# Two message-passing layers on a graph: edge maxima made in 13 pieces from flags computed early, and the last gathers' index tables copied by SP

## The reference

```python
h = jnp.maximum(_layernorm(x, axis=-1), 0.0)
# layer 0, with self loops appended to src, dst and ea
m = jax.nn.leaky_relu(x_l[src] + x_r[dst] + e_emb, NEG_SLOPE)
alpha = jnp.einsum('ehf,hf->eh', m, att)
amax = jax.ops.segment_max(alpha, dst, num_segments=n)
ex = jnp.exp(alpha - amax[dst])
denom = jax.ops.segment_sum(ex, dst, num_segments=n)
alpha = ex / (denom[dst] + SM_EPS)
out = jax.ops.segment_sum(x_l[src] * alpha[..., None], dst, num_segments=n)
...
# layer 1
msgs = x[src]
summed = jax.ops.segment_sum(msgs, dst, num_segments=n)
out = summed / jnp.maximum(deg, 1.0)[:, None] @ w_l.T + x @ w_r.T + b
```

## Time and profile before

| | us |
|---|---|
| median of 3 runs | 5774.85 |
| lowest and highest of the 3 | 5769.9, 5776.28 |
| the profiled execution: its time | 5776.47 |
| the profiled execution: its span | 5775.2 |

### The profile page before, as it was taken

One profiled execution on the slowest core, in us unless ns is written; L12 is line 12 of the kernel. 1 busy time (PEld: TensorE's weight loads), 2 busy tenths in 40 slices (PEclk: granted clock), 3 DMA queues, 4 the chain that ended last, 5 costly groups with the idle time before them and its releaser, 6 DMA issues. The chain is left out here.

```text
span 5775.2 us, 78491 instructions
## 1 busy us (share of the span) xinstructions
PE 4011.0 (69%) x16994; PEld 2971.1 (51%) x16995; DVE 3433.7 (59%) x8703; ACT 1190.3 (21%) x4516; POOL 3747.3 (65%) x3701
## 2 busy tenths in 40 slices
PE   5888888888888884699999998444444444334336
PEld 4766666666666663344444456343333333333336
DVE  7666666666666667899999999732222232222224
ACT  2111111111111110466666645200000000000001
POOL 4777777777777772465556540167777777777772
PEclk9999999999999997799999998555555555555555
DMA  8444444444444441243344431211111111111111
GB/s 129 131 133 131 128 131 130 130 130 132 129 130 131 128 130 52 90 112 112 110 111 111 112 83 30 58 24 26 26 26 26 26 26 26 26 26 26 26 26 33
DMA packets 620266, 477.65 MB, mean 83 GB/s; under 512 B 439032, under 2 KB 447352, under 8 KB 619820
## 3 DMA queue, kind: packets, MB, share of 16 engines
q1 hardware_dynamic: 452074, 254.69, 17.3%
q0 software_dynamic: 104800, 108.55, 10.7%
q10 hardware_dynamic: 63202, 112.44, 5.3%
HBM read 350.08 MB, written 125.20 MB: 82 GB/s over the span
## 5 line engine op out<-in xcount | busy, mean ns | idle before, releaser
L509 POOL DMA_INDIRECT ZR<-hD,mS x1664 | 1590.7, 956 | 563.9 <-issue 488.9
L1268 POOL DMA_INDIRECT BIG<-h2D,mS x1564 | 1475.9, 944 | 706.1 <-issue 468.3
L1292 PE MATMUL PS<-BIG,ZR 128*128 x3328 | 809.5, 427 | 1150.4 <-SPq L1245 524.8
L1292 PEld LDWEIGHTS PS<-BIG,ZR 128*128 128x128 f32 x3328 | 738.9, 328 | 1221.1 <-issue 656.1
L539 PE MATMUL PS<-Wz,R 128*128 128x264 f32 x3328 | 1057.2, 400 | 80.1 <-issue 79.5
L567 DVE SCALAR_TENSOR_TENSOR PS<-PS,a 128x528 f32<-128x528 f32 x832 | 596.3, 717 | 798.8 <-PE PS L540 795.0
L804 PE MATMUL PS<-R,ZR 128*128 128x329 f32 x3328 | 1024.8, 469 | 24.0 <-DVE ZR L739 18.4
L540 PE MATMUL PS<-BIG,R 128*128 x3328 | 1028.8, 391 | 0.0
L1311 DVE TENSOR_TENSOR BIG<-BIG,PS 128x64 f32 x1664 | 363.4, 218 | 916.8 <-PE PS L1292 747.1
L790 POOL TENSOR_TENSOR R<-ZR,R 128x768 f32<-128x768 f32 x416 | 615.9, 1480 | 418.7 <-ACT R L776 416.8
L818 DVE TENSOR_TENSOR BIG<-BIG,PS 128x329 f32 x1664 | 814.0, 489 | 11.3 <-PE PS L804 7.2
(11 more groups left out here) (252 smaller groups left out, 2355.1 us busy)
## 6 DMA issues: line engine op xcount, KB each, us to landing
zD<-ZR ACTq DMA_DIRECT2D x416, 256.0 KB, 2.2
ZR<-zD SPq DMA_DIRECT2D x416, 256.0 KB, 2.6
R<-relD SPq DMA_DIRECT2D x105, 512.0 KB
ZR<-ea SPq DMA_DIRECT2D x1664, 32.0 KB
ZR<-hD,mS POOLq DMA_INDIRECT x1664, 2.5
BIG<-h2D,mS POOLq DMA_INDIRECT x1564, 2.4
AL<-hD SPq DMA_DIRECT2D x28, 224.0 KB, 2.8
lmS<-lmD SPq DMA_DIRECT2D x106, 32.0 KB, 1.8
```

What stands on the lines that cost most here:

```text
L509: Q.indirect_dma_start(zring[:, j % 32, 0, :], None, hD, bass.IndirectOffsetOnAxis(mS[:, j // 16, j % 16:j % 16 + 1], 0)).then_inc(hs[q], 16)
L1268: Q.indirect_dma_start(BIG[:, j * F:j * F + F], None, h2D, bass.IndirectOffsetOnAxis(mS[:, (j // 16) % 4, j % 16:j % 16 + 1], 0)).then_inc ...
L1292: ins = P.matmul(bank3(j // 4)[:, j % 4, :], oh[:, (j // 4) % 4, j % 4, :], rows, start=True, stop=True)
```

## The change

**Preparation.** SP stores metaS behind relD and keyD instead of ahead of them, and no longer loads D. The flags (key differs from the last edge's) are computed inside the table product: ACT loads the keys again in tiles of 130 at pair KEYS = 14 (`keys_again`, which waits for the stores of keys and tables), DVE compares, scales and reduces them at pairs 18 to 20 (`flags`), PE and ACT turn and keep them at pairs 21 to 25, ACT's queue stores them at pair 27 and loads at pair 36 the flags of chunks (FLG, 6657 columns, the size of D) and their minima (cmin), which DVE reduces once ahead of sweep 1.

**Edge maxima.** ACT copies by column in 13 pieces and moves the turned pieces; DVE scans each piece as it comes, starting from the last column of the one before. The exchange between chunks is shorter: the flags' minima are there already, and DVE reads PE's result where it is. The second forward scan and the first backward scan are over the whole row. The second backward scan is in 13 pieces (`maxima`), each followed, one piece later, by PE's turn back and by `exponents`: DVE subtracts and masks straight from PSUM, ACT takes the exponential and writes zeros over what is no longer needed. The store of the maxima to lmD follows all pieces. The first loads of sweep 2's destinations stand ahead of the barrier, and behind the store only 3328 columns each are left to zero on DVE and POOL.

**Sweep 3.** SP, in `landings3`, issues a DMA of 16 columns of the index table into mS when it has seen a piece land (flows i3). ACT only copies mR. The wait of PE by register (1291) is as before.

```diff
-    dma(S, metaS.rearrange("a p c -> p a c"), MS.rearrange("p (a c) -> p a c", c=16), dM)
+    sources_turned = sa.n
...
+    S.wait_ge(sa.s, sources_turned)
+    dma(S, metaS.rearrange("a p c -> p a c"), MS.rearrange("p (a c) -> p a c", c=16), dM)
...
+    def keys_again():
+
+        dK.wait(A)
+        dM.wait(A)
+        dma(A, K3, bass.AP(kf.tensor, 0, [[128, 128], [128 * 128, 13], [1, 130]]), dKL)
+
+    def flags(step):
+
+        if step == 0:
+            dKL.wait(V)
+            v(V.tensor_tensor(F3, K3[:, :, 1:130], K3[:, :, 0:129], ALU.not_equal))
+        if step == 1:
+            v(V.tensor_scalar(G2, F2, BIGNEG, None, ALU.mult))
+        if step == 2:
+            v(V.tensor_reduce(tmid, G3[:, :, 1:128], AX.X, ALU.min))
+            for t in range(2):
+                sv.on(V.tensor_tensor(tmin[:, t, :], tmid, G3[:, :, 128 * t], ALU.min))
+            sv.wait(P, A)
...
+        dma(A, flagD[:, 0:NS * 128].rearrange("o (k p e) -> (o p) k e", p=128, e=128), G3[:, :, 0:128], dFl)
+        sa.wait(A)
+        dma(A, fminD.rearrange("t (k p) -> (t k) p", p=128), tmin_t, dFl)
+        dma(A, flagT, FT, dFl)
+
...
+        dFl.wait(A)
+        for t in range(2):
+            dma(A, cmin[:, t, :], bass.AP(fminD[t, :].tensor, NS * t, [[52, 32], [0, 4], [1, 52]]), dFm)
+        dma(A, FLG, bass.AP(ff.tensor, 0, [[CH, 32], [0, 4], [1, CH + 1]]), dD)
...
-    dK.wait(S)
-    dB.wait(S)
-    D, dD = BIG[:, 25998:25998 + CH + 2], dsem()
-    kf = keyD[0, :]
-    for h in range(4):
-        dma(S, D[h:128:4, :], bass.AP(kf.tensor, 0, [[CH, 32], [1, CH + 2]]), dD)
+    dFm.wait(V)
+    v(V.tensor_reduce(fmin, cmin, AX.X, ALU.min))
...
+    def by_column(q):
+        sa.on(A.copy(by_slot(CP[:, cols(q)]), AL4[:, 4 * q:4 * q + 4]))
+        at["cp", q] = sa.n
...
-    v(V.tensor_tensor(Fl, D[:, 1:CH + 2], D[:, 0:CH + 1], ALU.not_equal))
-    v(V.tensor_scalar(Fl, Fl, BIGNEG, None, ALU.mult))
...
-        v(V.tensor_copy(keep[:, 1:2], flags[:, 0:1]))
-        v(V.tensor_reduce(keep[:, 1:2], flags, AX.X, ALU.min))
-        v(V.tensor_tensor_scan(d(out), d(flags), d(data), BIGNEG, ALU.add, ALU.max))
...
+        sa.on(A.copy(AT[:, cols(q)], PS[:, q % 4, :]))
+        at["turned", q] = sa.n
+        if q + 2 < 13:
+            by_column(q + 2)
+        V.wait_ge(sa.s, at["turned", q])
+        before = FWD[:, 512 * q - 1:512 * q] if q else BIGNEG
+        v(V.tensor_tensor_scan(FWD[:, cols(q)], FLG[:, cols(q)], AT[:, cols(q)], before, ALU.add, ALU.max))
+
+    def from_other_chunks(col, t):
...
-    segmented_max(FWD, AT, Fl[:, 0:CH], False)
-    segmented_max(B, FWD, Fl[:, 1:CH + 1], True)
-    v(V.tensor_tensor(AT, AT, B, ALU.subtract))
+        v(V.tensor_copy(ini, PS[:, 6, 0:1]))
+
+    from_other_chunks(FWD[:, CH - 1:CH], 0)
+    v(V.tensor_tensor_scan(FWD, FLG[:, 0:CH], AT, ini, ALU.add, ALU.max))
+    nothing = bc(allone[:, 0:1], [128, 512])
     sv.wait(A)
-    sa.on(A.activation(AT, AT, ACT.Exp))
-    ex_rdy = sa.n
-    v(V.scalar_tensor_tensor(FWD, Fl[:, 1:CH + 1], 0.0, B, ALU.is_lt, ALU.mult))
...
+    for q in range(13):
+        sa.on(A.activation(AT[:, cols(q)], nothing, ACT.Copy, scale=0.0))
+    v(V.tensor_tensor_scan(LM[:, ::-1], FLG[:, 1:CH + 1][:, ::-1], FWD[:, ::-1], BIGNEG, ALU.add, ALU.max))
+    from_other_chunks(LM[:, 0:1], 1)
+    dFS.wait(V)
...
+    def maxima(q):
+
+        after = FWD[:, 512 * q + 512:512 * q + 513] if q < 12 else ini
+        if q < 12:
+            V.wait_ge(sv.s, at["max", q + 1])
+        b = FWD[:, cols(q)][:, ::-1]
+        sv.on(V.tensor_tensor_scan(b, FLG[:, 512 * q + 1:512 * q + 513][:, ::-1], b, after, ALU.add, ALU.max))
+        at["max", q] = sv.n
+        P.wait_ge(sv.s, sv.n)
+        if q + 4 < 13:
+            P.wait_ge(sv.s, at["lm", q + 4])
...
+        at["back", q] = sp.n
+
+    def exponents(q):
+
+        V.wait_ge(sp.s, at["back", q])
+        c, m = slice(4 * q, 4 * q + 4), by_slot(PS[:, q % 4, :])
+        sv.on(V.tensor_tensor(AL4[:, c], AL4[:, c], m, ALU.subtract))
+        sv.wait(A)
+        sa.on(A.activation(AL4[:, c], AL4[:, c], ACT.Exp))
+        sa.on(A.activation(FWD[:, cols(q)], nothing, ACT.Copy, scale=0.0))
+        sa.on(A.activation(FLG[:, 512 * q + 1:512 * q + 513], nothing, ACT.Copy, scale=0.0))
+        sv.on(V.tensor_tensor(LM4[:, c], m, bc(FS4[:, c].unsqueeze(3), [128, 4, 32, 4]), ALU.mult))
+        at["lm", q] = sv.n
+
+    maxima(12)
+    for q in range(11, -1, -1):
+        maxima(q)
+        exponents(q + 1)
+    exponents(0)
+    sv.wait(S, Q, A)
+    sa.on(A.activation(FLG[:, 0:1], nothing[:, 0:1], ACT.Copy, scale=0.0))
+    dma(S, lmD[:, 0:NHALF * 64], LM, dL)
+    dma(S, lmD[:, NHALF * 64:(NHALF + 2) * 64], LM[:, 0:128], dL)
+    sg.on(Q.memset(FS, 0.0))
+    v(V.tensor_copy(iota_ps, iota))
...
-    dL.wait(S, Q, V)
-    load_maxima(0, 0)
-    load_maxima(64, 1)
-    sg.on(Q.memset(BIG[:, 26000:29100], 0.0))
-    v(V.tensor_copy(iota_ps, iota))
-    v(V.memset(BIG[:, 13320:20000], 0.0))
-    v(V.memset(BIG[:, 29100:32300], 0.0))
-    sg.wait(V)
-    L2 = NS // 2
+    barrier()
...
+    dL.wait(S, Q)
+    load_maxima(0, 0)
+    load_maxima(64, 1)
+    sg.on(Q.memset(LM[:, 0:CH // 2], 0.0))
...
+    dL.wait(V)
+    v(V.memset(LM[:, CH // 2:CH], 0.0))
...
-                i3f.take(A)
-                A.copy(mS[:, half, :], sT[:, ds(i * 64 + 64 + 16 * half, 16)]).then_inc(i3_rdy.s, 1)
                 r3f.take(A)
                 A.copy(mR[:, half, :], rel3[:, ds(i * 64 + 64 + 16 * half, 16)]).then_inc(r3_rdy.s, 1)
-            close(i3f, r3f)
+            close(r3f)
...
+        def some(n, more):
...
-                    S.sem_inc(i3f.s, 1)
-
-        with S.Fori(0, NG3 // 64):
-            some(16)
-        some(NG3 // 4 % 16)
-        S.sem_inc(i3f.s, NHALF - 4 - NG3 // 16)
+                    if more is not None:
+                        S.dma_start(mS[:, q // 4, :], sT[:, ds(more + 4 * q - 12, 16)]).then_inc(i3[q // 4].s, 16)
+
+        with S.Fori(0, NG3 // 64) as i:
+            some(16, i * 64 + 64)
+        some(NG3 // 4 % 16, None)
...
-                    i3_rdy.take(Q)
+                    i3[(j // 16) % 4].take(Q, 16)
```

More of the change, by code:

```diff
@@ L630, in build @@
+    for t in range(2):
+        sp.on(P.matmul(PS[0:1, 5, t * 128:t * 128 + 128], fmin[:, t:t + 1], ident, start=True, stop=True))
+    sp.wait(V)
+    v(V.tensor_copy(fmins, PS[0:1, 5, 0:256]))
+    v(V.memset(edge, BIGNEG))
+    sv.wait(P)
+    def by_column(q):
+        sa.on(A.copy(by_slot(CP[:, cols(q)]), AL4[:, 4 * q:4 * q + 4]))
+        at["cp", q] = sa.n
     dD.wait(V)
     V.wait_ge(stored, 1)
-    v(V.tensor_tensor(Fl, D[:, 1:CH + 2], D[:, 0:CH + 1], ALU.not_equal))
-    v(V.tensor_scalar(Fl, Fl, BIGNEG, None, ALU.mult))
@@ L634, in build @@
-    sa.wait(V)
-    B = D[:, 0:CH]
-    ini = sc2[:, 0:1]
-    row = zall.rearrange("p s a f -> p (s a f)")
-    eR, fR, cR = row[0:1, 0:128], row[0:1, 128:256], row[0:1, 256:384]
-    def segmented_max(out, data, flags, backwards):
-        def d(ap):
-            return ap[:, ::-1] if backwards else ap
-        last = out[:, 0:1] if backwards else out[:, CH - 1:CH]
-        keep = sc2[:, 1:3]
-        v(V.tensor_copy(keep[:, 1:2], flags[:, 0:1]))
-        v(V.tensor_reduce(keep[:, 1:2], flags, AX.X, ALU.min))
-        v(V.tensor_tensor_scan(d(out), d(flags), d(data), BIGNEG, ALU.add, ALU.max))
-        v(V.tensor_copy(keep[:, 0:1], last))
+    by_column(0)
@@ L650, in segmented_max @@
+    def from_other_chunks(col, t):
         sv.wait(P)
[L651 to L652 removed]
+        sp.on(P.matmul(last_row, col, ident, start=True, stop=True))
         sp.wait(V)
[L654 to L656 removed]
+        e3, f3, c3 = by_chunk(last_row), by_chunk(fmins[:, 128 * t:128 * t + 128]), by_chunk(edge[:, 128 * t:128 * t + 128])
```

143 lines of the change are left out of this document (80 added, 63 removed).

## The result

The changed kernel took 5718.76 us in the median of 4 runs (5714.63 to 5719.68), the kernel before beside it 5773.14 (5769.9 to 5776.28): ratio 0.9904, 95% interval 0.9887 to 0.9922, faster by 54.4 us. Once more beside each other they gave 5719.0 and 5774.51, ratio 0.9904 (0.9887 to 0.992). The forecast was 5710 with a range of 5699 to 5731. The profiled execution took 5719.17 us, its span is 5717.8. In two other sessions every kernel, the kernel before too, took 6850 to 6970 us; they are told at the end, and no time of theirs is set against these.

What follows compares the result with a forecast made beforehand. Gathers bound sweep 1, begun late by DVE's gapless table product; DVE bounds the maxima and sweep 2, gathers sweep 3 with DVE held at its end. 5776.47 + 12.4 - 50.3 - 27.5 = 5711.1, median 5710, range 5699 to 5731.

Steps and rivals of the forecast that it cites:

- Part 1: Preparation: flag work 5.4, ACT's wait at pair 14 5.5 and DVE's wait for keys 1.5 add 12.4 us (8 to 22).
- the wait for the keys: Preparation, DVE waiting for ACT's second load of the keys: a loss of 1.5 us (0 to 5).
- ACT's stop: Preparation, ACT waiting at pair 14 until keys and tables are stored: 5.5 us, DVE losing as much (2 to 12).
- the one sentence that put PE's transposes beside DVE: Preparation: PE's 14 transposes and ACT's 6 copies lie beside DVE's work, PE the likelier to show.
- rival 1: Preparation costs 31.6 us instead of 12.4, as stores and loads queue up and ACT stops three times: 5729 us; chance 0.12.
- Part 2: Edge maxima between sweeps 1 and 2: first accumulation after 100.3 us against 150.6, so 50.3 us less (43 to 54).
- rival 3: Last 13 pieces of the maxima bound by a scan, PE, subtraction chain, 17.5 us more: 5727 us; chance 0.08.
- Part 3: End of sweep 3: DVE, no longer held by ACT's mR copies, ends near 5695 instead of 5722.5, 27.5 us less (22 to 29).
- Rival 2: Sweep 3: SP's small DMAs slow each gather by 0.013 us, 20 us in all: 5730 us; chance 0.05.
- the list of signs: What would show the forecast right or wrong, including sweep 3's last DVE add within 8 us of the last gather.
- Rival 4: Sweep 2: PE does not reach full clock, each slot costing 0.47 us more: near 6490 us, slower than before; chance 0.03.
- FLG's load: Start of sweep 1: loading the flags of chunks beside gathers and edge loads costs 0, with a bound of 9.2 us.

Runs made afterwards that it cites:

- both stops removed: Changed kernel with keys loaded at pair 17, flag steps from pair 22, flags turned six pairs behind them instead of three: 5708.61 us, ratio 0.9886.
- POOL's flags: Changed kernel with keys at pair 17, flags from 22, turned six pairs later, and comparison and scaling of the flags on POOL instead of DVE: 5730.73 us, ratio 0.9925.
- the second trace: Another trace of the same changed kernel, nothing edited; its table product ends at 148.78 us instead of 147.58.
- part 3 alone: The kernel before with only the sweep 3 change (SP copies the index tables by DMA, ACT only mR): 5746.19 us, ratio 0.9951.

## Why the prediction was right, and where it was off

- **What bounds the kernel**: right on sweep 1, wrong inside the table product. A later end of the table product moves sweep 1. In the kernel with both stops removed, the changed one and the one with POOL's flags the product's end moved by 9.2, 17.1 and 21.8 us against before, and the last score reduction of sweep 1 (at 2228.4 before) by 7.2, 17.0 and 19.9. But the prediction read DVE's merged row of 96 adds as an engine that is never free. PE was the one: busy 25.00 of 25.00 us, DVE 21.59. What counts there is how long PE stands still.
- **Part 1**, +12.4 forecast, +17.0 measured, inside the bounds of 8 to 22, but not by the forecast's sum (the adds end at 147.6, not near 143, and POOL's long run starts at 168.8, not near 163). Its flag work was sized right (5.06 and 0.25 for the reduction ahead of sweep 1, against 5.4) and its place was wrong: with no stop around it, the flag work and the wait for the keys, 6.7 us on DVE, held PE for 4.2. ACT's stop was taken at 5.5 and cost 4.0 (3.5 in the second trace). The wait for the keys was taken at 1.5 and was 0.58 (3.56). metaS behind the keys moved the landing by 1.4 us, not 3.4: what ends last is relF, whose issue takes 13.64 us now. **The step that failed is the one sentence that put PE's transposes beside DVE**: it looked at their busy time on an engine that had no time free (they cost 1.5), and not at the wait that `flags` puts on PE, which stood still for 5.65 us until DVE was done, and then ran at the lower clock. Moving that wait gave back 3.9 us. ACT's DMA issues, which the sum took at nothing (rival 1 had them at 5), are another 2.2. That the total came near is in part luck: the flag work was priced too high, the waits on PE too low.
- **Part 2**, -50.3 forecast, -49.6 measured. Counted as in the forecast, from 0.94 us behind DVE's last instruction of sweep 1, the maxima are complete at 83.9 us (82.5 forecast: the way in 3.2 instead of 2.6, the first 13 scans 17.06 instead of 16.3, the last pieces 31.2 instead of 30.8), the store 9.5 (9.9), from there to the first accumulation 7.5 (7.9). DVE never waited for PE in a piece, so rival 3 did not come.
- **Part 3**, -27.5 forecast, -27.2 in the trace of the changed kernel and in that of part 3 alone. Rival 2 did not come in the ordinary sessions. The last add ends 9.3 us after the last gather starts, not within 8 as the list of signs has it; the forecast's own sum gives 9.1 there, so the sign was written wrong and the sum was right.
- **Sweep 2** was taken as unchanged; it is 3.3 us longer (none in the kernel with part 3 alone). At its start one add more comes at the slower spacing (0.5 us); the rest is spread over the loop and has no name in the trace. The same loop took 1030.0 to 1030.5 us in the three traces without parts 1 and 2, 1033.4 to 1034.2 in ten with them, and 1038.3 with POOL's flags, so it belongs to the program and not to the run. What of the program it is was not tried.
- **Rival 4** did not come: the first four accumulations stand 1.1 us apart, then the clock rose.

```profile
2300.00:2332.00 32.00, 14.51 (x52) 9.31 (x52) 31.42 (x41) 20.90 (x38) 0.62 (x1) 0.50 0.00 0
2341.00:2350.00 9.00, 3.13 (x6) 2.09 (x7) 6.55 (x17) 5.16 (x24) 7.09 (x4) 0.50 0.59 163
2350.00:2360.00 10.00, 10.00 (x35) 6.65 (x35) 9.10 (x30) 6.98 (x32) 6.56 (x6) 0.93 0.33 106
```

From 0.50 to 0.93 in this stretch, as at the start of sweep 2 before: one slot more at the lower of its two levels (0.5 is 1.2 GHz), about 0.5 us. In the 13 pieces, bursts of 1.12 us every 2.37, the clock was 0.50: it had been there in the whole-row scans ahead, 0.50 with PE busy for 0.9 of 30 us, and it did not rise. The Trainium skill (TensorE: Matmul & The Clock Gate, HAM oscillation) says that waits between bursts of matmuls let the clock fall back each time. The low clock through the pieces agrees with it; sweep 2 is another case, since PE has no pause there.
- **FLG's load** beside sweep 1: taken at 0. POOL's run starts 21.2 us after the table product's end in the changed kernel and 20.0 before, and a second such load adds some 1.5. So 0 to 1.5 rather than 9.2. The bound that the prediction also drew from the Trainium skill (DMA: Bandwidth & Descriptors, Issuing engines are not separate DMA queues) was far too high here. Both kernels have 24 gathers behind them when POOL stalls, and its run goes on 20 to 21 us after the product's end in either; that this lead is what hides the load is argued, not tried.

The forecast was 9 us low, in the traces 4.6 of it in part 1, 3.3 in sweep 2, 1 in parts 2 and 3.
